# A decoder kernel: the long convolution's first group and the second group's key products put into the first attention's last group, in one block for all stages

## The reference

```python
x = x + _L0_attn_ref(_layernorm(x), ...)                  # attention, 16 heads of 16, low-rank updates on q, k, v, o
x = x + _L0_xattn_ref(ctx_2048, ctx_2048, _layernorm(x), L0_xattn_ssm_kernel, L0_xattn_D, 8)
x = x + _L0_ffn_ref(_layernorm(x), ...)                   # experts with low-rank updates
x = x + _L1_attn_ref(_layernorm(x), ...)                  # causal attention, 16 heads of 128
x = x + _L1_xattn_ref(_layernorm(x), ctx_2048, ...)       # linear attention
x = x + _L1_ffn_ref(_layernorm(x), ...)                   # mixture of experts
```

```python
kv = jnp.einsum('bhil,bhjl->bijhl', k_, v_)               # k and v are both the context
y = jnp.fft.irfft(rfft(kv) * rfft(ssm_kernel))[..., :L]   # a causal convolution in time
out = y + kv * D
out = jnp.einsum('bijhl,bhil->bjhl', out, q_)             # q is the normed x
```

## Time and profile before

| | us |
|---|---|
| median of 3 executions | 1004.58 |
| lowest and highest | 1002.87, 1007.49 |
| the profiled execution, its own time | 1005.1 |
| its span, first to last instruction | 1003.3 |
| TensorE busy | 944.8 (94%) |
| VectorE busy | 639.6 (64%) |
| ScalarE busy | 483.2 (48%) |
| GpSimd busy | 262.2 (26%) |

### The profile page before, as it was taken

How to read it: one execution, slowest core, us unless ns; L and a number is a source line. 1 busy time by engine, 2 the same in 40 slices (tenths; PEclk the granted TensorE clock), 3 DMA queues, 4 the chain that set the end, 5 groups by cost and what they waited for, 6 DMA issues and landing times.

```text
span 1003.3 us, 19775 instructions
## 1 busy us (share of the span) xinstructions
PE 944.8 (94%) x7441; PEld 815.2 (81%) x7441; DVE 639.6 (64%) x1376; ACT 483.2 (48%) x1613; POOL 262.2 (26%) x239
## 2 busy tenths in 40 slices
PE   5999997999888999999999999999999998999877
PEld 4777775999767888988888889888889976777757
DVE  5778896788976576544545456444564467687853
ACT  3888875433225555444444344444444453554431
POOL 2556774651531222201211111111111123110000
PEclk9999999999999999999999999999999999999979
DMA  8000000001102111100000000000000132000002
GB/s 297 19 2 2 2 2 1 23 1 64 43 3 85 42 49 58 53 1 2 1 1 2 2 1 1 1 1 1 1 1 1 54 122 85 2 2 2 1 1 85
DMA packets 12301, 28.02 MB, mean 28 GB/s; under 512 B 1937, under 2 KB 7345, under 8 KB 11569
## 3 DMA queue, kind: packets, MB, share of 16 engines
q1 hardware_dynamic: 11488, 26.55, 7.6%
q10 hardware_dynamic: 720, 0.20, 0.1%
HBM read 24.65 MB, written 2.10 MB: 27 GB/s over the span
## 4 chain that ended last, share of the span: by engine, by line
PE 73%; DVE 5%; ACT 2%; issue 1%; POOL 0%; DVEq 0%; ACTq 0%
PE bank L42 15%; PE bank L43 14%; PE bank L44 14%; PE bank L1446 6%; PE bank L1395 5%; PE bank L1436 3%; PE bank L1946 2%; PE bank L835 2%; PE bank L1959 2%; PE bank L813 2%; PE bank L814 2%; PE bank L815 2%; PE bank L143 2%; PE bank L2408 1%; PE bank L1936 1%
## 5 line engine op out<-in xcount | busy, mean ns | idle before, releaser
L1370 POOL TENSOR_TENSOR wa_prob<-wa_prob,wa_rsum 128x512 f32<-128x512 f32 x64 | 75.6, 1182 | 424.8 <-DVE wa_rsum L1623 424.8
L1527 ACT ACTIVATE wa_prob<-wa_prob,wa_negmax 128x128 f32<-128x128 f32 x256 | 100.0, 391 | 16.7 <-DVE wa_negmax L1612 16.4
L42 PE MATMUL bank<-norm_xT_hi,wide_hi 128*128 128x512 f32 x256 | 106.0, 414 | 1.6 <-DVE norm_xT_lo L154 1.6
L1657 DVE TENSOR_TENSOR le_w_or_z_lo<-bank,le_w_or_z_hi 128x512 fp32r<-128x512 f32 x64 | 44.2, 691 | 94.8 <-ACT le_w_or_z_hi L1568 94.1
L44 PE MATMUL bank<-norm_xT_hi,wide_lo 128*128 128x512 f32 x256 | 101.3, 396 | 0.0
L43 PE MATMUL bank<-norm_xT_lo,wide_hi 128*128 128x512 f32 x256 | 101.1, 395 | 0.0
L1548 ACT COPY wa_v<-bank 128x512 f32<-128x512 f32 x64 | 37.5, 585 | 126.6 <-PE bank L44 126.5
L523 ACT ACTIVATE v_or_conv<-bank,la_negmax 128x128 f32<-128x128 f32 x256 | 90.4, 390 | 3.6 <-DVE la_negmax L586 2.4
L1535 ACT COPY wa_q<-bank 128x512 f32<-128x512 f32 x64 | 37.5, 586 | 98.3 <-PE bank L44 98.3
L1618 DVE COPY wa_k<-bank 128x512 f32<-128x512 f32 x64 | 44.2, 691 | 62.7 <-PE bank L44 62.6
L281 POOL TENSOR_TENSOR v_or_conv<-v_or_conv,la_rsum 128x512 f32<-128x512 f32 x64 | 66.5, 1039 | 57.7 <-DVE la_rsum L591 57.7
(11 more groups left out here) (313 smaller groups left out, 2482.0 us busy)
## 6 DMA issues: line engine op xcount, KB each, us to landing
h_or_w<-in_wide_w SPq DMA_DIRECT2D x11, 512.0 KB, 4.3
li_em_w<-in_em_w SPq DMA_DIRECT2D x1, 4096.0 KB, 14.5
x<-in_x SPq DMA_DIRECT2D x4, 512.0 KB, 4.7
lc_kt<-in_ctx_rev SPq DMA_DIRECT2D x1, 2048.0 KB, 10.4
lc_toep<-in_toeplitz SPq DMA_DIRECT2D x1, 2048.0 KB, 14.7
out_x<-x SPq DMA_DIRECT2D x8, 256.0 KB, 2.6
le_raw<-in_wide_w SPq DMA_DIRECT2D x3, 512.0 KB, 6.4
li_kt<-in_ctx_rev SPq DMA_DIRECT2D x1, 1536.0 KB, 7.7
```

Of the source, the lines that this page charges most:

```text
L42: nc.tensor.matmul(out, a[0], b[0], start=start, stop=False, skip_group_check=True)
L1370: nc.gpsimd.tensor_tensor(prob[:, s], prob[:, s], rsum[:, s, :].unsqueeze(2).to_broadcast([P, G, P]), ALU.mult).then_inc(prob_ok, 1)
L1527: last = nc.scalar.activation(prob[:, s, j, :], prob[:, s, j, :], ACT.Exp, bias=negmax[:, s, j:j + 1], scale=SCALE, accum_out=sums[:, s, j ...
L1657: nc.vector.tensor_tensor(z[1][:, t % 2, :], b_z[:, :], z[0][:, t % 2, :].bitcast(F32), ALU.subtract).then_inc(z_lo, 1)
```

## The change

**On TensorE.** The first group's convolution moves into steps 50 to 65 of the attention, one head at the end of each (`conv_head`). All heads go through one bank, b_p[0], which the last group's steps leave unused. Head h + 1 starts when head h is copied.

**On ScalarE and VectorE.** In the step behind, ScalarE copies the even heads and VectorE the odd ones (`conv_copy`), into y. On ScalarE the copy stands ahead of the exponentials, on VectorE ahead of the copy of the turned probabilities. VectorE also makes the second group's statistics in steps 58 and 59.

**On GpSimd.** All of the second group's products, the squares too, are 16 pieces, one a step from step 49.

**Between the stages.** The attention's program stands at the head of the one block; the clearing of semaphores and the meeting of all engines behind it are gone. Twenty events are semaphores shared by several stages (`common`); later stages count on from where the earlier ones ended, and increments that only set a base are left out. TensorE's next stage begins with the transposes of the first group's normed x: the first four wait for the copied heads, the others for the attention's last update. SP loads the small weights of the next stage once the attention's own weights are split. q and k are two tensors each, and values and probabilities lie at the end of `v_or_conv`, so that y's first half is free earlier.

```diff
+        CONV_AT = N - U + 2
+        def conv_due(n, after):
+            h = n - after - CONV_AT
+            return h if 0 <= h < CONV_H else None
+        def conv_read(eng, heads):
+            if heads > 0:
+                eng.wait_ge(conv_act, (heads + 1) // 2)
+            if heads > 1:
+                eng.wait_ge(conv_vec, heads // 2)
...
+            def conv_head(h):
+                if h == 0:
+                    pe.wait_ge(v_ok, 2 * NG)
+                    pe.wait_ge(skip_ok, CONV_H)
+                    pe.wait_ge(kk_ok[0], 2 * CONV_C)
+                conv_read(pe, h)
...
+                nc.tensor.matmul(lo, same, early, start=True, stop=True, skip_group_check=True)
+                nc.tensor.matmul(hi, same, late, start=True, stop=False, skip_group_check=True)
+                nc.tensor.matmul(hi, across, early, start=False, stop=True, skip_group_check=True)\
+                    .then_inc(conv_ps, 1)
...
+                h = conv_due(n, 0)
+                if h is not None:
+                    conv_head(h)
...
+                h = conv_due(n, 1)
+                if h is not None and h % 2 == 0:
+                    act.wait_ge(conv_ps, h + 1)
+                    conv_copy(nc.scalar.copy, h).then_inc(conv_act, 1)
                 if n + 2 < N:
                     exps(n + 2)
...
+                h = conv_due(n, 1)
+                if h is not None and h % 2 == 1:
+                    dve.wait_ge(conv_ps, h + 1)
+                    conv_copy(nc.vector.tensor_copy, h).then_inc(conv_vec, 1)
                 if n < N:
                     keep_probT(n)
...
+                if n >= SECOND:
+                    if n == SECOND:
+                        pool.wait_ge(v_ok, 2 * NG)
+                    conv_piece(1, *PIECES[n - SECOND])
...
+            def turn_first():
+                for part in attention_done.conv_ok:
+                    pe.wait_ge(*part)
+                pe.wait_ge(norm.s_xn, norm.done(0))
+                norm.turn_chunk(pe, 0, 0, b_n[0])
+                pe.wait_ge(*attention_done.x_ok)
+                norm.turn_chunk(pe, 0, 1, b_n[1])
...
-            conv(0)
-            turn(0)
+            turn_first()
             for i in range(NG - 1):
...
-            squares(1)
-            keep_conv(0)
             norm.scalar_hi(act, 0, xT)
...
-            vector_pairs(1)
-            norm.vector_stats(dve, 1)
             apply(1)
...
-            stage_lora_attention(pr)
-            pr.release_semaphores()
+            attention, attention_done = lora_attention(pr)
```

More of the change, by code:

```diff
@@ L58, in sem, with common @@
         return self.sems[-1]
+    def common(self, name):
+        if name not in self.shared_sems:
+            self.shared_sems[name] = self.sem(name)
+        return self.shared_sems[name]
     def release_semaphores(self):
@@ L628, in extra @@
                         norm.vector_apply(dve, due, range(G // 2, G))
+                    if due == NG and u == NEXT_AT:
+                        dve.wait_ge(x_ok, 2 * G)
+                        norm.vector_stats_first(NG + 1)
+                    if due == NG and u == NEXT_AT + 1:
+                        norm.vector_stats(dve, NG + 1, G // 2)
                 else:
@@ L782, in gpsimd_program @@
             norm.enter_stage(1, 0, b_n)
-            for i in range(1, NG):
-                if i >= 2:
-                    pool.wait_ge(c_ps, (i - 1) * NGR)
-                    pool.wait_ge(norm.s_xn, norm.done(i - 1))
+            for i in range(2, NG):
+                pairs_free(pool, i)
+                pool.wait_ge(norm.s_xn, norm.done(i - 1))
                 pairs(nc.gpsimd, i, range(VECTOR_D, C)).then_inc(kk_pool, 1)
@@ L908, in shifted @@
                 qv = xT[:].rearrange("p a (bh c) -> p (a bh) c", c=C)
-                dve.wait_ge(c_ok, (i + 1) * NGR)
+                if i == 0:
+                    for part in attention_done.conv_ok:
+                        dve.wait_ge(*part)
+                else:
+                    dve.wait_ge(c_ok, i * NGR)
                 dve.wait_ge(norm.s_hi, DC * norm.done(i))
@@ L948, in long_conv @@
     last = (NG - 1) * G
-    done = ConvDone(bank_free={2: (x_ok, last - 2), 3: (x_ok, last)}, products_read=(c_ps, NG * NGR),
+    done = ConvDone(bank_free={2: (x_ok, last - 2), 3: (x_ok, last)}, products_read=(c_ps, (NG - 1) * NGR),
                     slots_read=(slot_ps, NG * C),
@@ L1503, in group @@
                         project(it, t)
-            for event in (s_ps, t_ps, z_ps, o_ps):
-                pe.sem_inc(event, BASE)
+            pe.sem_inc(z_ps, BASE)
             pe.wait_ge(norm.s_lo, DC * norm.split(0))
@@ L1581, in group @@
                         high(SPLIT_AT[t])
-            for event in (exp_ok, q_ok, v_ok):
-                act.sem_inc(event, BASE)
             high(0)
@@ L1912, in values @@
             pe.wait_ge(kt_lo, t + 1)
[L1913 removed]
+            wait(pe, v_ok, V_DONE + n)
             for c in range(DC):
```

313 lines of the change are left out of this document (170 added, 143 removed).

## The result

The changed kernel takes 997.21 us (median of 13 executions, 994.55 to 999.16); the kernel before, in 13 executions beside it, 1004.19 us. The ratio is 0.9926, 95% interval 0.9906 to 0.9946: 7.0 us or 0.74% faster. The forecast was 995.9 us, with a range of 993.4 to 1000.6.

A forecast was written before the change was run, and what follows sets the result against it. TensorE was taken to bound the kernel. Rebuilding step 50 to the second convolution saved 9.66 us, less 1.0 for waits: 8.7 us off the median of 1004.58 gave 995.9 us, range 993.4 to 1000.6.

The forecast's parts named there:

- What bounds the stretch: Steps 50 to 63: TensorE's own work bounds, pairs of steps about 4.4 to 5.3 us, TensorE busy over 95%.
- The sum: Step 50 to second group's convolution: 33.72 + 0.60 + 0.81 + 0.75 + 0.44 = 36.32 us, against 45.99 before.
- The bank's handover: Ahead of head 15, straight behind head 14 in the same bank: seeing it, copy and way back, 0.6 us.
- The end itself: Attention's end: last projection 0.81 us, x updated and way back 0.75, four transposes not hidden 0.44.
- At no cost: Second group's products and statistics, first group's x, SP's small weights some 120 us earlier, kept semaphores: all free.
- The clock: Last group and first convolution: the gain of 9.7 us at most includes what two low-clock stretches cost, not priced separately.
- The range's upper end: Whole kernel: 1000.6 us, from 3.9 us of waits instead of 1.0, the low clock and the scatter.
- (1): Last group's steps: single bank paces, six late ScalarE copies cost TensorE 6 us; gain 3.7, time 1001; chance 0.13.
- (2): Pairs of steps: the handover closes a loop of 6.0 us or more, kernel slower, 1006 to 1009; chance 0.04.
- (3): Steps 54 and 55: GpSimd's products block VectorE's normalising of x, TensorE loses 1.7 us, 997.6; chance 0.10.
- (4): Junction between the stages: clock falls, 3.5 us at half speed cost 1.75; median 997.6; chance 0.05.
- (5): Later stages: one waits for something that did not move and gives the gain back, 1004.6; chance 0.06.

The follow-up runs named there:

- the second trace: The changed kernel as it is, run and traced once more beside the kernel before: 996.44 us, ratio 0.9935.

## Why the prediction was right, and where its sizes were off

**What bounds the stretch.** Right. The heads sit in TensorE's waits of the last group: from step 50 into step 63 TensorE is busy 98.7%, pairs of steps up to step 59 take 4.54 and 5.2 to 5.3 us (forecast: about 4.4 to 5.3), heads given twice cost nearly their full work, and with the heads moved back nothing of the gain is left (1.0018 against 0.9926 and 0.9935).

**The sum.** The forecast had 36.32 us at the least from step 50 to the second convolution and took 1.0 for waits; measured are 38.12, so 1.8 in place of 1.0. Counted from start to start, as the forecast did, five terms make that up:

- Changes between kinds of matmul, 0.8 us. A head's first matmul behind a weighing or a wait costs 0.32 to 0.35 us instead of 0.245, twelve times, 1.2 in all; the transposes behind a head give back 0.05 eight times (0.53 for 0.58).
- The second group's statistics, 0.5 us. Head 10, in step 60, starts 0.47 us late, behind VectorE's copy of head 9 (rows below).
- The bank's handover ahead of head 14, 0.35 us. The forecast priced it ahead of head 15 alone, at 0.60; but head 14 has only the last weighing, 0.36, between itself and head 13. VectorE was idle for 1.28 us before that copy (177.32), so it isn't late; the handover takes that long.
- The same ahead of head 15, 0.66 us instead of 0.60.
- The transposes of step 62, 0.14 us, behind GpSimd.

VectorE's queue in step 59, and the head that waits for it:

```profile
167.72 0.74 DVE L123 BATCH_NORM_STATS2 norm_stats<-x 128x6 f32<-128x256 f32 x2
168.50 0.18 DVE L127 BATCH_NORM_AGGREGATE norm_meanvar<-norm_stats 128x2 f32<-128x6 f32 x1
...
169.08 0.66 DVE L653 TENSOR_REDUCE la_negmax<-bank 128x4 f32<-128x512 f32 x1
169.66 0.45 DVE L279 COPY v_or_conv<-bank 128x288 f32<-128x288 f32 x1
...
170.25 0.48 PE L448 MATMUL bank<-v_or_conv,lc_toep 128*128 128x144 f32 x2 [0.40 <-DVE v_or_conv L279]
```

The statistics hold VectorE from 167.72 to about 169; the maximum and the copy come behind them, while head 9 ended near 168.9. The same wait of 0.40 or 0.41 us is there in the second trace and in the one with zero fills, so it isn't the products. With the heads one step earlier the copy at this place is ScalarE's, and the wait is gone; with two steps it is VectorE's again, and the wait is back at 0.40. No run left the statistics themselves out.

The end itself was right: projection 0.86 (0.81), from there to the second convolution 1.18 (0.75 + 0.44).

**At no cost.** Half right. Beside the heads the second group's products cost 0.1 us in the stretch, the statistics 0.5 by the reading above. In a loop without the heads the products made two waits for GpSimd longer by 0.5 us each; what that costs in time stays open. The prediction counted products and statistics as free because they had been free in the later stage; what they cost is decided where they stand now, by what TensorE has to do meanwhile. SP's small weights are issued 158 us earlier (16.65, before 174.94) and not 120, and nothing waits for that.

**The clock.** The forecast had it in the sum, since it rebuilt the stretch at the full clock, but gave it no number of its own. It deserves one. In the windows before, the last group ran at a mean of 0.94 over 27 us and the first convolution at 0.87 over 13.5: at half speed for 3.2 and 3.5 us, half of which is lost, 3.4 us in all. That is an upper estimate, since in the last group a part may have gone into waits. The idle products show that it depends on what TensorE does in the waits. The same can be read from the times. Over the 216 executions whose clock is on record, those of one kernel are 0.76 us longer for each 0.001 that their mean granted clock is lower (least squares within the kernels). The kernel before ran from 997.7 us (0.990) to 1009.9 (0.975), 1003.4 at 0.984 on average over 82 executions; the changed one 996.9 at 0.986 over 22. By that slope, which is a correlation and no experiment, the difference at equal clock is about 4.5 us, and 2 us of the 6.5 are clock.

**Luck.** The profiled execution came out at 996.0, where 996.4 was forecast, but not by the forecast's way: its stretch gained 7.87 us and not 8.7, it began 0.68 us later, and the later stages were 1.9 us shorter, at a higher clock. The gain of the medians, 7.0 us, is 1.7 under the forecast. The range's upper end is added up wrongly: with 3.9 us of waits, the low clock at 1.75 and a scatter of 1.5 it is 1002.1; 1000.6 leaves the scatter out.

**Rivals.** (1) The bank doesn't pace the loop in the changed kernel: of its three waits, 1.17 us in all, one is in the loop and two are behind it. The late copy (+1.1 us in the trace) and the heads behind the transposes (+6 us) show how near it is. (2) did not happen: pairs of steps stay at 5.3 us or less. (3) The Trainium skill, SBUF — State Buffer, section "Who interferes with whom", says that GpSimd and a two-port instruction of VectorE block each other. The trace agrees in part: one normalising took 866 ns beside a product, the median stays 404, and without the products the longest is 407. The two pairs are 0.7 us longer in all and not 2, and the price on the path, 1.7 us in the forecast, is nothing that shows: VectorE was busy only 26.0 of 31.5 us. (4) The clock is 1.00 at the junction; it didn't fall with a pause of 1.43 us there either. (5) Nothing is given back: from the second convolution to the end the changed kernel took 812.0 and 809.5 us, before 813.9.

## What to carry to other kernels

Waits of TensorE of half a microsecond, spread over many steps, are a place for independent matmuls from the next stage: 11.8 us of them made a kernel 7 us shorter, and a part of that, by estimate 2 us, came from a clock that no longer fell. Count 0.1 us for a matmul of 128x144 behind a weighing, and a handover of the bank wherever two fillers stand with less than 0.6 us of other work between them. Check not only the busy share of the engines that empty the bank but where their copy stands between its neighbours: moving the heads by part of a step cost 6 us, and statistics ahead of a copy half a microsecond. Give such fillers the earliest steps that their inputs allow, so that none is left behind the last step.

## What the runs showed that I had not expected

- The time of a single kernel on one core is spread over 12 us, and most of that goes with the granted clock: 997.7 us at a mean of 0.990, 1009.9 at 0.975. A loop with many short waits is one place where the clock falls: in the kernel before it fell at 161 us, behind waits that were each 0.77 us or shorter. The same last group had 0.89 over 32 us with waits, and 1.00 with 7.8 us of idle products in them, in the same time (46.4 and 46.1 us up to the second convolution).
- A head's first matmul behind a weighing of 128*32 takes 0.35 us to the next, behind a projection 0.24; in the kernel with each head twice, its second set behind the first takes 0.25.
- GpSimd's fills of the same tiles with zeros took 0.38 us on average, its products 0.74, and only beside the products was VectorE's normalising stretched (866 ns; 407 at most beside the fills).
